# Gates summed by a scan on VectorE, half-row products, and two scalings on GpSimd, in one fused attention and linear-attention kernel

## The reference, cut to what matters

```python
q1, k1, v = x @ Wq, x @ Wk, x @ Wv                       # 512 wide
q2 = x @ Wqa @ Wqb                                        # through 64 features
k2 = softmax((x @ Wka @ Wkb) per head)                    # through 64 features
gk1 = log_sigmoid(x @ Wg1a @ Wg1b + bg1) / 16             # gates of the dense part
gk2 = log_sigmoid(x @ Wg2a @ Wg2b + bg2) / 16             # gates of the routed part
g  = cumsum(gk) in a chunk; qg = q*exp(g); kg = k*exp(-g) # then products with a running state
o  = o_dense + o_sparse
o  = o * rsqrt(mean(o*o per head) + eps) * norm_w
z  = x @ Wga @ Wgb                                        # through 64 features
out = x + (o * z * sigmoid(z)) @ Wo
```

## Time and profile before

| what | us |
|---|---|
| median of 3 runs | 1186.25 (1185.54 to 1187.19) |
| the profiled execution | 1185.8 |
| its span in the profile | 1184.5 |
| PE busy in the span | 1127.1 (95%) |
| DVE, ACT, POOL busy | 988.8, 903.2, 673.1 |
| one steady turn | 34.34 |

### The profile page before, as it was taken

The page is one execution under the profiler, slowest core; times in us unless marked ns, Lnnn a source line. Parts: engine busy times, 40 slices in busy tenths (PEclk is TensorE's granted clock), DMA queues, the critical chain, the costliest instruction groups (busy, mean ns, idle before and its releaser), DMA issues.

```text
span 1184.5 us, 30782 instructions
## 1 busy us (share of the span) xinstructions
PE 1127.1 (95%) x11936; PEld 918.7 (78%) x11936; DVE 988.8 (83%) x2729; ACT 903.2 (76%) x2290; POOL 673.1 (57%) x706
## 2 busy tenths in 40 slices
PE   3779999999999999999999999999999999999986
PEld 2557888887888888788888877888888788888764
DVE  4667998888989898898988888998988899988542
ACT  2587878878887778878778887878788788887751
POOL 4365655566555456665555666555566655555453
PEclk9689999999999999999999999999999999999998
DMA  6332122122212222222122122212212221222011
GB/s 166 132 112 57 45 63 60 49 57 80 58 40 55 59 58 54 67 60 64 48 62 58 40 65 66 65 37 78 61 43 56 57 61 40 55 55 53 16 26 24
DMA packets 79177, 71.14 MB, mean 60 GB/s; under 512 B 33017, under 2 KB 63679, under 8 KB 79030
## 3 DMA queue, kind: packets, MB, share of 16 engines
q1 hardware_dynamic: 78598, 68.22, 22.1%
q10 hardware_dynamic: 432, 0.95, 0.2%
HBM read 37.89 MB, written 13.94 MB: 44 GB/s over the span
## 4 chain that ended last, share of the span: by engine, by line
PE 75%; ACT 12%; POOL 3%; DMA 3%; SPq 3%; DVE 2%; issue 1%; DVEq 0%; POOLq 0%
PE F L391 16%; PE TM L714 6%; PE F L767 5%; PE F L794 4%; PE F L830 4%; PE F L755 4%; PE F L385 4%; PE TM L385 3%; PE SA L702 3%; PE TM L721 3%; PE F L778 3%; PE F L1072 2%; PE F L811 2%; PE TM L731 2%; ACT ZABS L1851 2%; PE F L737 2%
## 5 line engine op out<-in xcount | busy, mean ns | idle before, releaser
L784 POOL TENSOR_TENSOR DEC<-EG 128x20 f32<-128x20 f32 x28 | 7.7, 275 | 278.1 <-DMA EG<-EGP 278.1
L709 DVE CUSTOM_DVE_ANT_0 SA<-SA,LNC 128x154 f32<-128x154 f32 x512 | 146.2, 347 | 12.5 <-PE SA L702 12.3
L695 DVE TENSOR_REDUCE PACKED<-HOT 128x19 int32<-128x1216 bf16 x64 | 92.3, 1442 | 0.3
L714 PE MATMUL TM<-CONST,EXPS 128*128 128x128 f32 x512 | 91.4, 302 | 1.1 <-ACT OT L1705 0.8
L2115 POOL TENSOR_TENSOR LS<-LS,ZABS 128x1024 f32<-128x1024 f32 x28 | 66.6, 2378 | 36.7 <-ACT ZABS L1858 36.7
L714 PEld LDWEIGHTS TM<-CONST,EXPS 128*128 128x128 f32 x512 | 72.1, 209 | 10.9 <-issue 4.8
L709 DVE DVE_READ_ACCUMULATOR2_ANT MAXS<- 128x1 f32 x512 | 72.2, 141 | 0.0
L2100 POOL TENSOR_TENSOR QM<-QD,ISEXPT 128x1024 f32<-128x1024 f32 x28 | 66.4, 2372 | 1.7 <-DMA QD<-QG 1.7
L1428 DVE TENSOR_TENSOR STATE<-STATE,F 128x512 f32<-128x512 f32 x28 | 19.3, 688 | 56.8 <-PE F L824 56.8
L2104 POOL TENSOR_TENSOR QM<-QD,ISEXPT 128x1024 f32<-128x1024 f32 x28 | 66.4, 2372 | 0.0
L2103 POOL TENSOR_TENSOR AT<-AT 128x1024 f32<-128x1024 f32 x28 | 66.4, 2370 | 0.0
(11 more groups left out here) (528 smaller groups left out, 3891.8 us busy)
## 6 DMA issues: line engine op xcount, KB each, us to landing
QD<-QG SPq DMA_DIRECT2D x128, 128.0 KB, 2.4
QS<-q_dram SPq DMA_DIRECT2D x64, 192.0 KB, 3.4
q_dram<-QPARTS SPq DMA_DIRECT2D x32, 192.0 KB, 2.1
XA<-x_dram SPq DMA_DIRECT2D x32, 128.0 KB, 2.2
QS<-q_dram SPq DMA_DIRECT2D x32, 128.0 KB, 2.4
XB<-x_dram SPq DMA_DIRECT2D x32, 128.0 KB, 3.2
out_dram<-OUT SPq DMA_DIRECT2D x32, 128.0 KB, 1.7
EG<-EGP SPq DMA_DIRECT2D x128, 4.0 KB, 1.8
```

Of the source, the lines that this page charges most:

```text
L695: return dve.tensor_reduce(PACKED[:, r], HOT[:, r, :], AX.X, ALU.add)
L709: last = dve.tensor_tensor_reduce(s, s, LNC[t % 2][:, :], -1.0, LARGE, ALU.add, ALU.min, out[:, h:h + 1])
L714: pe.transpose(TA[:, cols(hh)], exps[:, 0:P, hh], ident)
```

## The change

1. The sum of the dense gates is no product any more. Two `tensor_tensor_scan` on DVE, one over each half of 256 columns (the first backwards), add them along tokens; RESET holds a zero at each head's start. For that `z_features` makes the first gates' pre-activations with features on partitions and tokens along columns: four bf16 products of 128 columns in place of one of 512. `cum_half` is gone, and EP and EN1 are exponentials of GSUM in SBUF, not of PSUM.
2. `half_pairs` and `half_rows`: q2, z and k2 are made of 64-row operands, the even ones from partitions 0 to 63 and the odd ones from 64 to 127, into two banks. For this HQ, HID2 and HID1 are copied to the other half of the partitions by three DMAs of 64 x 128 a tile (HQ, HIDG, HIDK).
3. The scaling of k2 by KS and OG*RMS go from DVE to POOL.
4. Turns are cut elsewhere: x's norm, the picks' comparison and scores of the first four heads, q1 and k1 and the scans stand a turn earlier by the letter of their stage (l for a, a for b, c for d), at the end of a turn. LAG is 5 and FILL 6; stage e has no work of its own. The lists of all engines are written in another order.

```diff
+        def z_features():
+            r = slice(0, len(Z_SLABS) * GR)
+            for p in range(NP):
+                last = pe.matmul(by_half[:, p], ZW[r, 0, cols(p)], ZS[r, 0, :], start=True, stop=True)
+            return last
+        def half_pairs(out, w, *srcs):
+            for p in range(NP // 2):
+                for n, src in enumerate(srcs):
+                    r = slice(DK * n, DK * n + DK)
+                    last = pe.matmul(out[:, n, cols(p)], w[r, cols(p)], src[r, :], start=True, stop=True)
+            return last
+        def half_rows(out, x0, x1, w):
+            for n, src in enumerate((x0, x1)):
+                r = slice(DK * n, DK * n + DK)
+                last = pe.matmul(out[:, n, :], src[r, :], w[r, :], start=True, stop=True)
+            return last
...
-            pairs(D0, lambda k, p: LS3[d % 2][:, 0, cols(p)], lambda k: cum_half).then_inc(s_d_g1_ps, 1)
...
-            pairs(D2, lambda k, p: WQKB[:, cols(p)], lambda k: HQ[d % 2][:, :]).then_inc(s_d_q2_ps, 1)
...
+            half_pairs(MIDD, WQKB, HQ[d % 2], HQ[d % 2]).then_inc(s_d_q2_ps, 1)
...
+            half_pairs(MIDS, WG, HID2, HIDG).then_inc(s_c_zg_ps, 1)
...
+            half_rows(MIDS, HIDK, HID1, WKB).then_inc(s_c_k2_ps, 1)
...
+            dve.tensor_tensor_scan(GSUM[:, 0:HD // 2][:, ::-1], RESET[:, :], LS3[c % 2][:, 0, 0:HD // 2][:, ::-1], 0.0, ALU.mult, ALU.add).then_inc(s_d_scan0, 1)
+            dve.wait_ge(s_d_scan0, c + 1)
+            dve.tensor_tensor_scan(GSUM[:, HD // 2 + 1:HD + 1], RESET[:, :], LS3[c % 2][:, 0, HD // 2:HD], 0.0, ALU.mult, ALU.subtract).then_inc(s_d_scan1, 1)
...
+            pool.tensor_tensor(K2[d % 2][:, :, :], K2[d % 2][:, :, :], KS[:, 3, :].unsqueeze(2).to_broadcast([P, H, DK]), ALU.mult).then_inc(s_c_soft_pool, 1)
...
+            pool.wait_ge(s_d_osg, d + 1)
+            pool.wait_ge(s_e_rms, d + 1)
+            pool.tensor_tensor(flat(OG[:, :, :]), flat(OG[:, :, :]), RMS[:, :], ALU.mult).then_inc(s_e_rmsog, 1)
```

More of the change, by code:

```diff
@@ L169, in program @@
         HID2 = sb("HID2", [P, P])
+        HIDG = sb("HIDG", [P, P])
+        HIDK = sb("HIDK", [P, P])
         LOGIT = sb("LOGIT", [P, NE])
@@ L461, in pool_pads @@
             pool.memset(CREST[:, :, :, :], 0.0)
+            pool.memset(GSUM[:, :], 0.0)
+            pool.memset(RESET[:, :], 1.0).then_inc(s_ones, 1)
+            pool.wait_ge(s_ones, 1)
+            pool.memset(RESET[:, 0:HD // 2:DK], 0.0)
             pool.memset(COUNTI[:, :], 0)
             pool.memset(WEIGHT[:, PICKS - 1:PICKS], 0.0)
[L464 to L467, removed]
+            pool.memset(EXPS[:, :, NKV:NPAD, :], 0.0).then_inc(s_pads, 1)
         def pool_ones():
@@ L826, in state_outputs, with ffn_out, pe_first_tiles @@
             return last
-        def ffn_out():
+        def ffn_out(out, og):
             for p in range(NP):
-                last = pe.matmul(D1[:, D:2 * D], OG[:, p, :], WO[:, p, :], start=p == 0, stop=p == NP - 1)
+                last = pe.matmul(out, og[:, p, :], WO[:, p, :], start=p == 0, stop=p == NP - 1)
             return last
-        def pe_first_tiles(l, a, b, c, d):
+        def pe_first_tiles(l, a, b, c, d, e):
+            if d >= 0:
+                pe.wait_ge(s_c_sigm, d + 1)
+                pe.wait_ge(s_d_q1, d + 1)
+                gate_products(LS3[d % 2], CUME[d % 2]).then_inc(s_d_g2_ps, 1)
+            if c == 0:
+                pe_v_rest()
             if b == 0:
                 pe_c_rest()
[L836 to L851, removed]
-                pairs(D0, lambda k, p: LS3[d % 2][:, 0, cols(p)], lambda k: cum_half).then_inc(s_d_g1_ps, 1)
[L853 to L866, removed]
+            if c >= 0:
+                pe.wait_ge(s_c_xm, c + 1)
+                transposes(C0, XM[:, :], KD).then_inc(s_c_xmt_ps, 1)
             if b >= 0:
@@ L984, in pe_first_tiles @@
                 attn_out().then_inc(s_b_y_ps, 1)
+            if l == 0:
+                pe.wait_ge(s_const, 16)
+            pe.wait_ge(s_a_xn, l + 1)
+            if l >= 3:
+                pe.wait_ge(s_c_soft, 5 * l - 13)
+            transposes(spare, XN[:, :], KD).then_inc(s_a_xt_ps, 1)
             if d >= 0:
@@ L1033, in pe_tiles @@
+            v_product(XMT[c % 2]).then_inc(s_c_v_ps, 1)
+            pe.wait_ge(s_d_tokens, 2 * d + 1)
+            transposes(D0, flat(KG2T[:, :, :]), NP).then_inc(s_d_k2gt_ps, 1)
             values(b, 1, PT[1]).then_inc(s_b_values, 1)
-            pe.wait_ge(s_d_at1, d + 1)
             inner(KG2T, QG2).then_inc(s_d_a2_ps, 1)
+            pe.wait_ge(s_c_hidg, 16 * c + 16)
+            pe.wait_ge(s_d_tokens, 2 * c)
+            half_pairs(MIDS, WG, HID2, HIDG).then_inc(s_c_zg_ps, 1)
+            pe.wait_ge(s_b_exps2_2, b + 1)
@@ L1145, in pe_last_tiles @@
                 kv_products(VM[d % 2])
+            if b < TILES:
+                pe.wait_ge(s_b_exps2_2, b + 1)
+                scores(b, 3).then_inc(s_b_scores, 1)
+            if c < TILES:
+                pe.wait_ge(s_c_zslabs, 48 * c + 48)
+                pe.wait_ge(s_c_silu, 4 * c + 1)
+                z_features().then_inc(s_c_z0_ps, 1)
+            if b < TILES:
+                values(b, 1, PT[1]).then_inc(s_b_values, 1)
+            if d < TILES:
                 pe.wait_ge(s_d_at, d + 1)
@@ new lines, in act_first_tiles @@
+            if d >= 0:
+                act.wait_ge(s_d_o_ps, d + 1)
+                act.activation(RMS[:, :], D0, ACT.Square).then_inc(s_d_sq, 1)
+            if a == 0:
+                act_v_first()
+            if b == 0:
+                act_k_rest()
+            if b >= 0:
+                act.wait_ge(s_b_values, 4 * b + 4)
+                act.activation(OT[:, 3, :], OUTS, ACT.Copy).then_inc(s_b_ot, 1)
+            if c >= 0:
+                act.activation(ZABS[:, 2, :], SG[c % 2][:, :], ACT.Abs).then_inc(s_c_silu, 1)
+                act.wait_ge(s_c_silu, 4 * c + 2)
+                act.activation(LS3[c % 2][:, 2, :], SG[c % 2][:, :], ACT.Relu, scale=-1.0)
@@ new lines, in act_first_tiles @@
+            if a >= 0:
+                act.wait_ge(s_a_counts, 7 * a + 7)
+                act.activation(LN[:, :], COUNT[:, 0:NKV], ACT.Ln, bias=const("tiny")).then_inc(s_a_lncount, 1)
+            if d >= 0:
+                act.wait_ge(s_d_ms_ps, d + 1)
+                act.activation(RMS[:, :], D2, ACT.Ln, bias=eps).then_inc(s_d_norm, 1)
+                act.wait_ge(s_d_norm, d + 1)
+                act.activation(RMS[:, :], RMS[:, :], ACT.Exp, scale=-0.5).then_inc(s_e_rms, 1)
+            if b >= 0:
+                act.wait_ge(s_b_ont_ps, b + 1)
+                act.activation(flat(ONT[:, :, :]), TA[:, 0:D], ACT.Copy).then_inc(s_b_ont, 1)
@@ L2110, in pool_tiles @@
+            pool.wait_ge(s_d_osg, d + 1)
+            pool.wait_ge(s_e_rms, d + 1)
+            pool.tensor_tensor(flat(OG[:, :, :]), flat(OG[:, :, :]), RMS[:, :], ALU.mult).then_inc(s_e_rmsog, 1)
+            pool.wait_ge(s_c_silu, 4 * c + 4)
+            pool.tensor_tensor(LS3[c % 2][:, 2, :], LS3[c % 2][:, 2, :], ZABS[:, 2, :], ALU.add).then_inc(s_c_ls2, 1)
             pool.wait_ge(s_a_lncount, a + 1)
```

1953 lines of the change are left out of this document (1001 added, 952 removed).

## The result

The changed kernel takes 1159.16 us (1155.66 to 1159.72, 4 runs), the kernel before 1186.55 in the same session: a ratio of 0.976, 95% interval 0.974 to 0.978, 27 us less. 1146 was forecast and the range was 1116 to 1166. The direction is right; 13 us of the forecast gain of 40 are missing.

What follows compares the result with a forecast made beforehand. PE's work was taken as the bound: 34.34 us a turn falls to 32.26, plus 1.0 waiting, called 33.2; 28 turns save 32 us, ramps and end 8, so 1185.8 - 40 = 1146 us, range 1116 to 1166.

Steps and rivals of the forecast that it cites:

- PE's list: PE's work in a steady turn, taken as the bound: 34.34 less 0.94, 0.70 and 0.44, giving 32.26 us.
- The halves: 64-row products on PE: q2 and z 0.55 each, saving 0.35 each; k2 0.52, saving 0.44 us.
- DVE's stretch: DVE from STATE to Q, linking PE's `state_outputs` to its next `gate_products`: 9.42 us plus S, against PE's 10.65.
- S: What the scans add to DVE's stretch: 2.10 us, up to 2.64; PE waits for anything above 1.11.
- The exclusion on the port: A two-SBUF-input DVE operation and a POOL one block each other; expected scan, POOL's product (1.26), scan in sequence.
- The scan: One 256-column scan on DVE: 0.42 us, up to 0.69; half throughput would add about 0.27.
- The second, smaller link: From ON's start through OG and POOL's product to `ffn_out`: 3.0 us against PE's 2.85; 0.5 together, overlapping the other wait.
- The forecast's 1.0 of waiting: PE's wait per turn for DVE's stretch, in front of `gate_products` or XN's transposes: about 1.0 us.
- K*KS: Scaling of k2 on POOL at the turn's start: 1.26 us, hidden, costs nothing; DVE loses about 0.66.
- the half-rate scan's 1161: Within rival "Half gained" (chance 0.20; turn 33.7 to 34.0, 1164 us): scans at half throughput alone give 1161.
- QM was late on POOL: QM on POOL could delay `state_outputs`: priced at 0 in the sum, up to 0.5 us a turn in the range.
- the rival "slower": Chance 0.09: scan much slower than a plain operation; over 0.2% slower from 1.05 us a scan; at 1.2, 1199 us.

Runs made afterwards that it cites:

- e10: The `e9` kernel with Q on DVE also made ahead of the sum of K's exponentials: 1136.0 us, ratio 0.958, turn 32.78.
- e9: The changed kernel with OG*RMS back on DVE, between the two scans; K*KS stays on POOL: 1136.8 us, ratio 0.959, turn 32.88.
- e1: The changed kernel with POOL's two index operations moved behind its product OG*RMS: 1153.7 us, ratio 0.972, turn 33.39.
- e8: The changed kernel with each scan replaced by a plain product of the same operands, leaving out the sums: 1143.9 us, ratio 0.964, turn 33.12.
- e6: The changed kernel with K*KS back on DVE at the turn's start, OG*RMS left on POOL: 1168.2 us, ratio 0.984, turn 34.01.
- e5: The changed kernel with OG*RMS back on DVE, behind both scans; K*KS stays on POOL: 1145.4 us, ratio 0.965, turn 33.09.

## Why the prediction was right in direction and 13 us short

**PE's list: right, a little too short.** Forecast 32.26; in `e10` the turn of 32.78 has two visible waits left, the 0.23 for ON and 0.05 for the copy HIDG (1.4 us in 3 turns), so the list is 32.5. The gates' product is gone, 0.94 as said. The halves save less than the forecast's 0.35 each: q2 takes 0.65 (597.10 to 597.75; forecast 0.55), and the product of 128 rows ahead of it 1.03 instead of 0.89 (576.11 to 577.00): 0.11 saved. z, which stands behind a product of 64 rows, takes 0.57 and shortens that by 0.10: 0.43. k2 takes 0.63 (585.79 to 586.42; forecast 0.52), and `attn_out` behind it 0.97 in `e9` instead of 0.86: 0.22 of the forecast 0.44. The row of `inner` from which they were scaled has 64 rows on its own side only; the changes from one shape to the other were not taken from it. These savings add up to 1.70, 34.34 to 32.64; the last 0.1 down to 32.5 is spread over blocks in the new order and not taken apart. No run undoes the gates' sum or the halves; what they gave is read from these distances alone.

**DVE's stretch: the arithmetic right, the size S wrong, and so not the bound.** The forecast had 9.42 + S. Measured, STATE at 582.07 to Q's end at 593.56, less 0.72 idle, is 10.77; S, from the first scan's start to KS, is 586.92 - 585.56 = 1.36; the rest is 9.41. PE's side is 594.06 - 582.07 less 1.08 of waiting, 10.91 against 10.65 forecast. So S = 1.36 leaves PE no wait. In `e1` S is 586.51 - 584.14 = 2.37, inside what the forecast allowed (up to 2.64), and PE's waits make some 0.9 a turn (33.39 for 32.5), of which 0.24 stand in front of `gate_products`. Where the scans do enclose the product, the forecast's mechanism is there, if smaller than its formula gives (2.37 - 1.11 = 1.26). The step that failed is "POOL's OG*RMS becomes ready with DVE's OG, in the moment when the first scan starts": it is ready only with RMS from ACT, 0.5 later, and behind two index operations it got to the port after the second scan instead of before, in 24 of 27 turns.

**The exclusion on the port: right.** In `e1` a scan of 0.69 takes 1.74 beside a product of 1.27; in the kernel after the product takes 1.65 behind a scan. The one that issues first keeps its time, the other is blocked. The Trainium skill says so (SBUF — State Buffer, Who interferes with whom), and both traces agree, though neither loses quite the other's whole length: the scan 1.05 of 1.27. Which of the two comes first had to be worked out, from the waits of each.

**The scan: mis-sized.** 0.42 forecast, 0.69 measured, with 0.43 for the plain product of the same tiles (`e8`). The Trainium skill's rule that the built-in scan runs at half throughput (DVE: opcode table, instruction layouts, handler registers and perf-mode slots; Datapath and trigger behaviour) was set aside for want of a row; the trace agrees with it, 0.26 more each, and `e8` prices it at 15 us, which is the figure that the forecast gave beside that rule. It acts through POOL's product, though, and not through the stretch, so that the figures agree is luck.

**The second, smaller link: this was the bound.** It was priced at 0.5 and then dropped ("They add nothing until S is small"). From ON's start (584.30) to the product's end (588.07) it is 3.77 where the forecast had 3.0. From the first scan's start to the product's it is 0.86 for 0.42 (0.67 with the plain product of `e8`, so 0.19 is the scan's length; the rest is RMS and POOL's queue), and the product takes 1.65 for 1.26, held behind the second scan. The forecast's 1.0 of waiting is there as 1.08, 0.85 for POOL and 0.23 for ON, at another place and for another reason: that the sizes agree is luck. The turn is 33.60 against 33.26, which was rounded to 33.2: the list is some 0.25 longer and the waiting 0.08.

**K*KS: "costs nothing" was right for POOL, wrong for DVE.** That DVE loses 0.66 was "nothing to speak of" as a load. `e6` is 9 us slower without it, of which some 2.6 are PE's waits for HIDG, so the move is worth 6 to 9. With `e5` and `e9` the two halves of the move to POOL are told apart: K*KS gains that, OG*RMS on POOL loses 14 us against OG*RMS on DVE behind the scans and 22 against between them.

**Sum.** 28 turns at 0.74 are 20.7 us (32 forecast), ramps and end 5.7 of the span's 26.4 (8 forecast); the changed kernel has 27 steady turns, and counted with 27 it is 20.0 and 6.4.

The rivals: the half-rate scan's 1161 came nearest, in size; its path was another. QM was late on POOL in no way that PE felt (0.3 us in all). In the rival "slower" one step is off: by its own formula 0.2% is passed from a scan of 1.01 us on, not 1.05. At 0.69 that changes nothing.

## What to carry to other kernels

When work goes to another engine, list everything that its last operand waits for, and where it stands in both engines' queues; the port goes to whoever issues first, and in this kernel some 0.1 us decides it. Two chains that start at the same instruction don't cover each other: price both to their ends, and take the longer, before calling one "smaller". A wait in front of a product can be the image of a chain that stands without slack behind it (ON and k2): moving what is named in the wait then only moves the wait.

## What was not expected of the hardware

- A scan of 256 fp32 columns takes 0.69 us, the plain product of the same operands 0.43.
- In every turn of `e1` the second scan took 1.73 to 1.745 us, 1.05 more than alone; POOL's product OG*RMS took 1.27 there and, in most turns of the kernel after, 1.65. Both orders occur in one and the same kernel, 0.1 us apart.
- PE pays some 0.1 us where products of 128 rows and of 64 rows meet: the block ahead of q2 went from 0.89 to 1.03, the block behind k2 from 0.86 to 0.97, and where such a meeting went away, ahead of z, a block fell from 1.09 to 0.99. That the meeting is the cause is read from these three blocks; no run was made for it.
